# One token tile of the next unit turned ahead of each pair, the first unit's rows gathered into the output buffers, idle matmuls on a standing TensorE

## What is computed

```
x = x + tanh(g_xattn) * V' sigmoid(layernorm(x)' ctx / 16)      # per batch, K = V = ctx
t = rmsnorm(layernorm(x)) * norm_w
logits = t @ gate_w.T + gate_b ; top 4 of 16 experts ; softmax of the 4 -> G
h = t @ w1[e].T + b1[e]                     # 512 -> 1024, even columns a, odd columns b
act = min(a, 7) * sigmoid(1.702 a) * (clip(b, -7, 7) + 1)
y = act @ w2[e].T + b2[e]                   # 512 -> 512
out = x + tanh(g_ffn) * (layernorm(x) + sum over e of G[:, e] * y)
```

## Time and profile before

| what | us |
|---|---|
| median of three runs | 849.4 (849.01 to 851.18) |
| the profiled execution | 844.8 |
| its span, first to last instruction | 843.0 |
| PE busy in it | 770.3 (91%) |
| DVE, ACT, POOL busy | 503.6, 446.5, 311.6 |
| attention stage, to the last product with V | 0.8 to 138 |
| routing, table, first gathers | 138 to 180.8 |
| expert loop | 180.8 to 831 |

### The profile page before, as it was taken

How to read it: one execution, slowest core, us unless ns; L and a number is a source line. 1 busy time by engine, 2 the same in 40 slices (tenths; PEclk the granted TensorE clock), 3 DMA queues, 4 the chain that set the end, 5 groups by cost and what they waited for, 6 DMA issues and landing times.

```text
span 843.0 us, 16501 instructions
## 1 busy us (share of the span) xinstructions
PE 770.3 (91%) x3972; PEld 641.6 (76%) x3973; DVE 503.6 (60%) x1006; ACT 446.5 (53%) x771; POOL 311.6 (37%) x290
## 2 busy tenths in 40 slices
PE   5999998058999999999999999999999999999984
PEld 2555555047888899988888888898998988898873
DVE  2677675416676575566576665756556575746540
ACT  3455534025566564556557655646556565656540
POOL 0257665631324315242324323324333334325212
PEclk9999998559999999999999999999999999999997
DMA  8566653052577576347649655556535555544312
GB/s 290 180 199 217 208 167 113 5 137 75 130 210 168 108 221 162 62 130 206 138 148 229 174 108 126 148 135 154 145 60 150 108 151 139 150 124 75 37 25 38
DMA packets 107767, 117.00 MB, mean 139 GB/s; under 512 B 11808, under 2 KB 77344, under 8 KB 107744
## 3 DMA queue, kind: packets, MB, share of 16 engines
q1 hardware_dynamic: 88896, 77.32, 29.7%
q0 software_dynamic: 18848, 39.40, 23.8%
HBM read 88.06 MB, written 28.94 MB: 139 GB/s over the span
## 4 chain that ended last, share of the span: by engine, by line
PE 80%; DVE 7%; issue 4%; ACT 3%; POOL 2%; DMA 1%; DVEq 0%; ACTq 0%; POOLq 0%
PE ps L525 37%; PE ps L474 25%; PE ps L378 7%; PE ps L389 7%; PE ps L453 3%; POOL tab L1093 2%; DVE W1l L1028 1%; DVE uu L1017 1%; DVE hv L1019 1%; PE ps L406 1%; DVE bv L1015 1%; ACT hTh L698 1%; ACT bw L678 1%; PE ps L397 1%; DVE ps L988 1%
## 5 line engine op out<-in xcount | busy, mean ns | idle before, releaser
L525 PE MATMUL ps<-xTh,W1h 128*128 x768 | 257.8, 336 | 14.3 <-issue 7.9
L525 PE MATMUL ps<-xTl,W1h 128*128 x768 | 251.9, 328 | 0.0
L525 PE MATMUL ps<-xTh,W1l 128*128 x768 | 251.7, 328 | 0.0
L1175 POOL DMA_INDIRECT out<-ys,dgI x75 | 118.8, 1584 | 307.2 <-ACT ys L657 283.7
L525 PEld LDWEIGHTS ps<-xTh,W1h 128*128 128x128 f32 x768 | 145.7, 190 | 25.3 <-issue 20.3
L525 PEld LDWEIGHTS ps<-xTh,W1l 128*128 128x128 f32 x768 | 145.7, 190 | 5.5
L525 PEld LDWEIGHTS ps<-xTl,W1h 128*128 128x128 f32 x768 | 145.9, 190 | 5.0
L474 PE MATMUL ps<-W2h,hTh 128*128 x300 | 119.8, 399 | 7.7 <-DVE hTl L1023 7.7
L474 PE MATMUL ps<-W2l,hTh 128*128 x300 | 117.5, 392 | 0.0
L474 PE MATMUL ps<-W2h,hTl 128*128 x300 | 117.4, 391 | 0.0
L657 ACT ACTIVATE ys<-ps,dgI 128x512 f32<-128x512 f32 x75 | 51.7, 690 | 123.5 <-DVE ps L988 123.5
(11 more groups left out here) (130 smaller groups left out, 999.8 us busy)
## 6 DMA issues: line engine op xcount, KB each, us to landing
W1f<-in_wts SPq DMA_DIRECT2D x64, 512.0 KB, 4.7
W2f<-in_wts SPq DMA_DIRECT2D x32, 512.0 KB, 6.9
X<-in_x SPq DMA_DIRECT2D x8, 512.0 KB, 6.5
Kt<-in_ctx SPq DMA_DIRECT2D x8, 512.0 KB, 4.4
Vt<-in_ctxT SPq DMA_DIRECT2D x8, 512.0 KB, 4.0
rows<-tt SPq DMA_DIRECT2D x8, 512.0 KB, 3.0
out<-base SPq DMA_DIRECT2D x8, 512.0 KB, 3.0
b2s<-in_bias SPq DMA_DIRECT2D x16, 256.0 KB, 9.1
```

Source lines behind the costliest of these rows:

```text
L525: m = e.matmul(P_[i % 2][:, 0:32 * w], (W1h, W1l)[wl][:, i, 2 * k + h, :], (xTh, xTl)[xl][:, bass.ds(par, 1), k, 0:32 * w], start=(t == 0) ...
L1175: e.indirect_dma_start(out, bass.IndirectOffsetOnAxis(dgI[:, j, 0:1].bitcast(I32), axis=0), ys[j][:], None, compute_op=ALU.add).then_inc(d ...
```

## The change

Four edits. (1) On PE t0 stands ahead of pair 0, and t1 between pair 0 and the second layer; t2 and t3 stay. ACT and DVE take t0 up as the first of their unit (ACT behind `bcur`) and t1 behind the first gate and the first three steps. (2) The first unit's rows are gathered into `ys`, with row numbers in a tile of their own, `src0`, after a wait for the attention stage's last output (`a_base`), since `ys` lies on its buffer; the wait of POOL for the first four turns goes. (3) Seventeen matmuls on a constant stand ahead of PE's first score, five ahead of the first unit's first turn, one behind each of the first three turns and three behind the fourth. (4) DVE sets the constant tiles `ones` and `many` ahead of `hv`.

```
@@ PE
+            def run_idle(n):
+                for _ in range(n):
+                    e.matmul(ps[0][:, 0:256], idm, C[:, 0:256], start=True, stop=True)
+            e.wait_ge(v_ones, 1)
+            for _ in range(17):
+                e.matmul(RK[:], ones[:], many[:].unsqueeze(1).broadcast_to((128, 4, 128)), start=True, stop=True)
...
+            e.wait_ge(d_idx0, 16)
+            run_idle(5)
             for j in range(4):
-                e.wait_ge(d_g[j], 16)
-                turn_x(j, 1, P0[j])
+                e.wait_ge(d_first[j], 16)
+                turn_x(j, 1, ys, P0[j])
+                run_idle(1 if j < 3 else 3)
...
                 for i in range(4):
-                    if i == 0:
-                        e.wait_ge(e_xl, ready)
+                    turned_in(i)
+                    if i == 1:
+                        second_layer(e.snap(u * 4 + 4))
...
                     pick(WIDTHS)
-                    if i == 0:
-                        turned_in(0)
-                        second_layer(e.snap(u * 4 + 4))
-                    if i < 3:
-                        turned_in(i + 1)
@@ ACT (DVE alike, with hidden for gate)
+                turned_in(0)
                 by_width(lambda w: gate(0, w))
-                turned_in(0)
+                turned_in(1)
                 second()
-                turned_in(1)
@@ POOL
-            place(0, 1)
+            e.wait_ge(a_base, 2 * B)
+            e.tensor_copy(src0[:], idx[:, 0:4, :]).then_inc(e_src, 1)
+            e.wait_ge(e_src, 1)
             for j in range(4):
-                gather(j)
+                e.indirect_dma_start(ys[j][:], None, rows, bass.IndirectOffsetOnAxis(src0[:, j, 0:1].bitcast(I32), axis=0)).then_inc(d_first[j], 16)
...
-            e.wait_ge(e_tx, 4)
             place(row(nxt), 2)
```

More of the change, by code:

```diff
@@ L131, in build @@
         bcur = sb("bcur", [128, 3, 4])
+        src0 = sb("src0", [128, 4, 2])
         srcI = sb("srcI", [128, 4, 2])
@@ L218, in build @@
         d_g = [sem(f"d_g{j}") for j in range(4)]
+        d_first = [sem(f"d_first{j}") for j in range(4)]
         e_src, e_dg = sem("e_src"), sem("e_dg")
@@ L448, in pe, with turn_x @@
             e.matmul(LG[:, 64 + F_NT * NUP:64 + F_NT * NUP + NUP], ones[0:E, :], Q3[:], start=False, stop=True).then_inc(t_te, 1)
-            def turn_x(j, r, P_=PX):
+            def turn_x(j, r, from_=xg, P_=PX):
                 e.wait_ge(e_xl, r)
                 for c in range(4):
-                    m = e.transpose(P_[:, 128 * c:128 * c + 128], xg[j][:, 128 * c:128 * c + 128], idm)
+                    m = e.transpose(P_[:, 128 * c:128 * c + 128], from_[j][:, 128 * c:128 * c + 128], idm)
                 m.then_inc(e_tx, 1)
@@ L484, in pe @@
             for r in landed:
-                e.reg_mov(r, 16)
+                e.reg_mov(r, 0)
             e.reg_mov(turned, 4)
@@ L505, in turned_in @@
                         e.reg_add(landed[j], landed[j], 16)
-                        come, free = e.snap(landed[j], min_val=32, max_val=16 * NTILES), e.snap(turned, min_val=5, max_val=NTILES + 24)
+                        come, free = e.snap(landed[j], min_val=16, max_val=16 * NTILES), e.snap(turned, min_val=5, max_val=NTILES + 24)
                         e.wait_ge(d_g[j], come)
@@ L520, in part @@
                     def part(w):
+                        if i == 0:
+                            e.wait_ge(e_xl, ready)
                         for h, P_, q in ((0, PA, e_l1a), (1, PB, e_l1b)):
@@ L857, in low @@
                     e.tensor_tensor(W2l[:, 0, half2(c)], W2f[:, 0, half2(c)], W2h[:, 0, half2(c)].bitcast(F32), ALU.subtract).then_inc(e_lo2, 1)
+            e.memset(ones[:], 1.0)
+            e.memset(many[:], float(TE)).then_inc(v_ones, 1)
             for q in hv:
                 e.memset(q[:], 0.0).then_inc(v_zero, 1)
-            e.memset(ones[:], 1.0)
-            e.memset(many[:], float(TE)).then_inc(v_ones, 1)
             e.memset(MM[:, 0, 0, :], 0.0).then_inc(v_mm0, 1)
@@ L1113, in place @@
             def place(col, r):
-                e.tensor_copy(srcI[:], idx[:, col:col + 4, :] if isinstance(col, int) else idx[:, bass.ds(col, 4), :]).then_inc(e_src, 1)
+                e.tensor_copy(srcI[:], idx[:, bass.ds(col, 4), :]).then_inc(e_src, 1)
                 e.wait_ge(e_src, r)
```

## The result

The changed kernel takes 904.19 us (median of four, 898.89 to 905.1) against 849.2 for the kernel before: ratio 1.0629, 95% interval 1.0585 to 1.0674. That is 55 us slower where the prediction said 35.5; it lies inside the range of 866 to 905, at its edge. The profiled execution took 904.66, its span 902.9, so 59.9 more than the profiled one of before (844.8).

The account below looks back on a forecast made before the run. The prediction took PE, 80% of the chain, to bound the kernel, with the loop hardly waiting. Its terms, 16 + 17 + 7 - 3 - 5.5 - 2 + 6 = +35.5, put the median at 849.4 + 35.5 = 885 us, range 866 to 905.

Parts of the forecast that it names:

- ten wide units: Units with a wide pair 0: t1 waits for xTl, so each ends 1.2 to 2.4 us later, together +16 us.
- seven narrow units: Units with a narrow pair 0: t1 waits for xTl, losing 2.1 to 2.6 us each, together +17 us.
- the other units, late gathers: At the starts of units 9, 11, 17 and 19, t0 waits for its gathered rows: +7 us.
- behind the second layer: In five narrow units that end an expert, ACT no longer makes t1's xTh ahead of W1h: -3 us.
- clock in the loop: PE's stands in the loop bring four falls of its clock, 1.6 us each: +6 us.
- head and between stages: Idle matmuls speed the first scores (-2 us); separated turns and idle matmuls shorten unit 0 (-5.5 us).
- rival D: In the loop, ten clock falls, DVE's way round the full 1.08, 0.4 more per PE restart: 905 us, chance 0.16.
- The way to xTl: At a unit's start, DVE's W1l and then its way round its loop, taken as 0.9 us, set t1.
- rival B: In the loop, t1 is free but late gathers bind: 848 us, no change, chance 0.04.
- A: Rival: in the loop the splits keep up, no turn waits, only gains are left: 836 us, chance 0.06.
- C: Rival: DVE's way round its loop is short, ACT's way sets t1, the clock holds: 872 us, chance 0.22.
- E: Rival: idle matmuls don't help the clock; head and unit 0 give only 3 us: 890 us, sharing the forecast's 0.52.

Follow-up runs that it names:

- after_again: The changed kernel run once more, unaltered, beside the follow-up kernels: 902.16 us, ratio 1.0665 to the kernel before.
- two_early: The changed kernel with t0 in a PSUM bank of its own and tile 0 gathered as soon as t0 is read: 831.85 us, ratio 0.9838.
- both_ways: The changed kernel with quarter 3's W1l behind t0's xTl on DVE and t0's xTh ahead of the bcur copy on ACT: 892.7 us, ratio 1.0579.

## Why the prediction was right in sign and 20 us short

Read from the timelines of the two profiled executions, unit by unit (from the end of the unit before to the second layer's start, less pair 0 and less t1's own 0.35; from the second layer's end to the unit's end; lengths of the second layer and pair 0), the terms of the sum came out so, in us:

| term | priced | measured |
| --- | --- | --- |
| ten wide units | +16 | +20.3 |
| seven narrow units | +17 | +21.0 |
| the other units, late gathers | +7 | +13.3 |
| behind the second layer | -3 | -5.7 |
| clock in the loop | +6 | +15.0 |
| head and between stages | -7.5 | -4.0 |
| sum | +35.5 | +59.9 |

Every loss came out larger than priced and the head gave less in this execution; only the gain behind the second layer was larger. That the time lies inside the range owes something to luck: the interval of the ratio, 1.0585 to 1.0674, is 899 to 906 us on 849.2, across the end of the range, and the ratio of `after_again` would give 906.

- **Wide and narrow units.** The mechanism held: in 15 units t1 waits for xTl, 0.2 to 3.9 us, 1.3 or more in 13 of them. The size of the wait was nearly right too: W1l's end to xTl is 0.82 in four units and 1.17 in six, where I took 0.9; five have no W1l. What was left out is the restart: 0.75 us from t1 to the second layer instead of 0.35, 6.9 us over 17 units; for t1 it had a place only in rival D. In units 1 and 3 no row shows a wait at t1: t0 came 0.2 late, pair 0 began 0.9 to 1.0 later behind it than in the kernel before, and by then the split was done; a restart of 0.3 to 0.4 stood behind t1 all the same.
- **The way to xTl** was half wrong: I let DVE alone decide. ACT's way (0.9 to 1.5 us from hTh to bcur in these units, then 0.20, 0.41 and xTh 0.59) is as long, and where there is no W1l longer, so the "0.67 in this unit" that I carried over from unit 1 was an end and not the rule; and on DVE the way round, not W1l, is what takes the time.
- **Gathers.** Unit 9 was foreseen at 3.8 and stood 3.54. What failed is the step "Elsewhere the rows are there within 0.3 us of the start, or early": eleven waits came, not four, and those outside units 9, 11, 17 and 19 are 0.2 to 1.5 us long. Pair 0 began late behind t0 as well, 11.4 us over all units, for which the sum had no term (rival B had 4 x 0.4). But in the kernel before, where no turn stood ahead of it, pair 0 began late too, 10.0 us in all and nearly all of it in ten units, partly for ACT; in `two_early`, where t0 hardly waits, it is 8.3 us, for the most part in the same ten. So against the kernel before the late starts cost some 1.4 us and not 11.4; new are units 1, 2 and 3, with 0.9 to 1.0 each, and unit 7 with 0.65; several others are shorter than they were.
- **Behind the second layer.** Units 11, 13 and 19 gave back 0.6 each, as forecast; 17 and 21 gave 0.1. The units of two tiles, 10, 16, 18 and 22, gave 0.5 to 0.6 each and weren't priced. In `two_early` the same term is -6.1 and the other terms of the loop come to nothing, so this is where the order gains.
- **Clock.** Four falls were priced, nine came, of 1.3 to 2.5 us each. Of the eleven stands of 1.50 us or more ahead of t1 eight were followed by a slow second layer, of the two of 1.3 none; the prediction had kept the price to the longest. PE's busy time is 798 and not the 770 that I expected: 22 more in the loop, 15 of them slow clock, 13 of idle matmuls, 7 less elsewhere.
- **Head and unit 0.** The head gave 1.7 of its 1.8 us, as the earlier trace rows had it, and pair 0 ran at the fast clock, which I had refused to take. The Trainium skill (TensorE: Matmul & The Clock Gate, section What's actually happening) says that activity releases the slow clock; 7.13 against 8.85 agrees. The profiled execution lost some 3 us in the attention stage, where PE waited 2.4 in all for ACT's Sc; `after_again`, and the other kernels with the same code there, don't show this, and unit 0 of `after_again` ends 8.2 us earlier than before's. So the term was sized about right, and the -4.0 in the table is of one execution.
- **Of the rivals** A and B are out, C had its way of ACT right and its price wrong, E is out by the head; D, with many falls and restarts, was the nearest in size, 905, at a chance of 0.16; it had left out the extra gathers.

## What to carry to other kernels

Before a step is moved ahead, ask of each thing it waits for when that is ready, and price the way of every engine to it with the way round its loop; where two of them end together, taking time from one gives nothing. A wait that PE stands at costs more than its length: here 0.4 us of restart behind t1, and behind most of the longer ones the clock. Before a late start is put down to a new wait, look whether the kernel before has it too. An order that loses by two waits may win once what makes them is gone: here a second bank and an earlier gather turned +57 us into -13, of which the edits to the ends gave 5.

## What the runs showed of the hardware beyond this

The Trainium skill (Advanced Engine Details and Errata, section Control Flow Timing) gives 0.051 us for a branch and 0.108 for a compare-and-branch; one and two or three of these lie there, an estimate of 0.3 to 0.4. No run here shows what the rest is.
- From the last work of one turn of its loop to the first of the next, with no work between, DVE took 1.1 to 2.1 us (`both_ways`, hTl's end to xTl) and ACT 0.9 to 1.7 (the same run, hTh's end to xTh, but for one unit in which t0 itself was late).
- The releaser that a row names can be one that was done before: `both_ways` names xTh, 0.47 us after it had ended.
